# A graph network kernel on one core: TensorE enters the next pass inside the last steps of a pass, the last tile's weights are turned by TensorE, and passes 2 and 3 sum 256 columns

## The chip, the cores and the metric

One core of a Trainium2 chip. The metric is the device time of one execution, in microseconds (us). Three runs of the kernel before gave 2464.94, 2465.70 and 2465.91 us, median 2465.7 us.

## What is computed

Four graph layers over 6250 nodes with 128 features and 206250 edges. Every layer is normalised first and added to x (`layernorm` is over the features, without weights). Cut to what matters:

```
h = relu(layernorm(x));  x += segment_sum(w_edge * (sigmoid(h @ Wg + bg) * (h @ W0))[dst], src)
h = relu(layernorm(x));  x += segment_sum(h[src], dst) @ W1.T + b1
h = relu(layernorm(x));  m = [h[src], h[dst]] @ Wm + bm;  x += [h, segment_sum(m, dst)] @ Wu + bu
h = relu(layernorm(x));  e = Binv * segment_sum((h @ W3)[src], dst)
                         o = Dinv * segment_sum(e[dst], src) + b3
                         x += relu(gamma * batchnorm_over_nodes(o) + beta)
```

## The kernel before

The graph becomes a dense matrix of counts. The nodes are cut in 49 tiles of 128. **The build** makes, tile by tile, a 128 x 6272 strip of counts (how many edges go from node to node) and one of edge weights, by products of one-hot matrices on TensorE; ScalarE copies them from PSUM to `stage` (L1348 the counts and the high part of the weights, L1329 the low part of the weights). The counts are stored in DRAM (`counts_by_source`, 1.6 MB a tile). The weights of a tile (a high part and a low part, 49 blocks of 128 x 128 each) are turned into `wt` and multiplied with the gated rows `g_in`: this is layer 1, and it is done in the same stage, for a pair of tiles at a time (`sum_some`, L701 to L703, 16 groups of 3 target tiles, the last of 4; 3 matmuls of 128 columns for each target tile and source tile). VectorE adds each group into X (`add_some`, L1057).

**Four passes** then multiply the whole matrix of counts with rows of h: `step` on TensorE sums for each of the 49 tiles 49 matmuls (L804) of 258 columns: 128 of the high part of h, 128 of the low part and 2 extra ones (degrees). Pass 1 is layer 2, pass 2 layer 3, passes 3 and 4 layer 4. Only passes 1 and 4 read the two extra sums. Passes 1 to 3 load the counts of a tile with one DMA of 1.6 MB on the SP queue (L505, six slots, load j waits until tile j-6 is summed). Pass 4 needs the transposed matrix and loads two tiles at once with one DMA transpose (L542, three slots for pairs).

What orders the work around the change:

- The weights of tiles 0 to 47 are turned partly by DMA transposes on the SP queue (`hand_on`: L489, for each of the two parts a piece of 24 blocks and one of 17) and partly by TensorE (L725, 8 blocks a part, read out by ScalarE at L1358) inside the next tile's build. The last tile, 48, has no next tile, so all of its blocks go through the SP queue: L489 and then L499 (`rest_turned`). Its 147 matmuls are a group of their own (n = GROUPS - 1) behind the 294 of the pair ahead, and VectorE adds its 16 groups and takes the row statistics (`row_stats`, L1072) behind each.
- After the statistics come `norm` (L892 to L900), the split of h in two parts (L1286, L1101, L1103) and pass 1.
- A pass on TensorE is `tiles_loop(pe, step, 2)`: step j sums tile j, then turns the result of tile j-1 (L814, in pass 2 also L813), then multiplies that of tile j-2 with the layer's weights (L822; L825 and L826; L828). Steps 49 and 50 have only the latter two. ScalarE (`low`, `aggt`) and VectorE (`agg`, then X, the statistics and the next h, L1114 and L1124) follow; in passes 1 and 2 row j-5 of the next h is made at step j, so that VectorE and ScalarE have five more steps (49 to 53). The next pass begins when all 49 rows are there:

```
if ph > 1:
    pe.wait_ge(s(f"h_ready{ph}"), TILES)
```

- The sums of a pass alternate between PSUM banks 0 and 1 (`sum_bank`), and the two banks of tile 47 and 48 are free as soon as `low` and `agg` have read them.

## Time and profile before

| | |
|---|---|
| median of 3 runs | 2465.7 us (2464.94 to 2465.91) |
| profiled execution, its own time | 2461.69 us |
| its span | 2459.8 us |
| TensorE matmul busy | 2293.2 us, 93% |
| mean granted clock of TensorE | 0.978 of full speed |
| VectorE, ScalarE busy | 1444.7 us (59%), 1279.8 us (52%) |
| DMA moved | 569.80 MB, mean 232 GB/s |

The span is what the profiler's first and last instruction enclose; the execution's own time is 1.9 us more. In the span the build takes up to about 1234 us; pass 1 starts at 1241, pass 2 at 1541, pass 3 at 1864, pass 4 at 2137, and the last sum ends at 2435. "Busy" counts a matmul from its start to a modelled end, so that neighbours overlap; a rate is better read from start to start.

### The profile page before, as it was taken

The page shows a single profiled execution, that of the slowest core. Times are in us where ns is not written, and L with a number is a line of the kernel's source. Part 1 is how long each engine was busy: PE and PEld are TensorE (multiplying, and loading weights), DVE is VectorE, ACT ScalarE, POOL GpSimd, SP SyncE. Part 2 cuts the span into 40 slices and gives each one's busy share as a digit, 9 for nine tenths or more (in the row PEclk, how much of TensorE's full clock was granted, in tenths as well). Part 3 has the DMA queues.
Part 4 walks back from the last instruction along what each step waited for, and adds up shares of the span by engine and source line. Part 5 has one row for each costly group of instructions (what it writes and reads, how often), then busy time and mean ns, then how long its engine had stood idle before and what let it go on. Part 6 is the DMA issues. An engine that isn't in the chain of part 4 may idle for free.

```text
span 2459.8 us, 72172 instructions
## 1 busy us (share of the span) xinstructions
PE 2293.2 (93%) x28669; PEld 2025.0 (82%) x28669; DVE 1444.7 (59%) x3422; ACT 1279.8 (52%) x2875; POOL 57.0 (2%) x57
## 2 busy tenths in 40 slices
PE   3689999999999989999889998999998999998997
PEld 3469898998899889988768887888887888887886
DVE  8779999998899988989643233234333111222223
ACT  3689999999899989989342222222221000011112
POOL 3500000000000000000000000000000000000000
PEclk9799999999999999999989999999999999999998
DMA  7799999999999999999989999999998999999997
GB/s 188 182 213 195 201 212 207 209 210 200 189 208 208 196 203 195 205 197 205 226 202 291 290 290 290 248 261 257 258 261 214 291 290 290 264 252 241 269 268 188
DMA packets 1528563, 569.80 MB, mean 232 GB/s; under 512 B 869815, under 2 KB 1526971, under 8 KB 1528152
## 3 DMA queue, kind: packets, MB, share of 16 engines
q1 hardware_dynamic: 1524709, 559.04, 104.0%
q0 software_dynamic: 1200, 4.10, 0.6%
q8 instruction: 200, 3.28, 0.5%
q10 hardware_dynamic: 2370, 2.71, 0.4%
q14 instruction: 84, 0.68, 0.1%
HBM read 257.85 MB, written 92.19 MB: 142 GB/s over the span
## 4 chain that ended last, share of the span: by engine, by line
PE 63%; SPq 16%; ACT 9%; DMA 5%; issue 4%; DVE 3%; POOLq 1%; another core or an unknown queue 0%; POOL 0%; DVEq 0%; ACTq 0%
PE ps L804 35%; SPq L542 8%; SPq L489 5%; ACT stage L1348 4%; PE ps L732 4%; ACT stage L1329 3%; PE ps L733 3%; PE ps L734 3%; PE ps L701 3%; PE ps L702 3%; PE ps L703 3%; PE ps L709 3%; DMA wt<-stage 3%; SPq L486 2%; PE ps L725 1%
## 5 line engine op out<-in xcount | busy, mean ns | idle before, releaser
L1348 ACT CAST stage<-ps 128x784 f16<-128x784 f32 x784 | 657.4, 838 | 18.0 <-PE ps L734 10.5
L804 PE MATMUL ps<-Ha,a_tiles 128*128 128x258 f16 x4606 | 523.9, 273 | 7.2 <-DVE Ha L1124 7.2
L732 PE MATMUL ps<-hot_c,hot_r 128*128 128x98 f16 x3136 | 502.7, 210 | 13.5 <-DVE hot_c L1046 10.4
L804 PEld LDWEIGHTS ps<-Ha,a_tiles 128*128 128x128 f16 x4606 | 449.9, 98 | 73.5 <-DVE Ha L1124 7.6
L733 PE MATMUL ps<-hot_c,hot_r 128*128 128x98 f16 x3136 | 500.4, 210 | 0.0
L734 PE MATMUL ps<-hot_c,hot_r 128*128 128x98 f16 x3136 | 498.8, 209 | 0.0
L701 PE MATMUL ps<-g_in,wt 128*128 128x128 f16 x2401 | 426.9, 220 | 29.2 <-DMA wt<-stage 20.1
L1329 ACT CAST stage<-ps 128x392 f16<-128x392 f32 x784 | 405.1, 517 | 43.4 <-PE ps L709 40.8
L703 PE MATMUL ps<-g_in,wt 128*128 128x128 f16 x2401 | 426.9, 220 | 0.0
L702 PE MATMUL ps<-g_in,wt 128*128 128x128 f16 x2401 | 426.9, 220 | 0.0
L1046 DVE TENSOR_TENSOR hot_c<-hot_c,meta 128x1568 f16<-128x1568 f16 x392 | 379.2, 967 | 0.0
L732 PEld LDWEIGHTS ps<-hot_c,hot_r 128*128 128x128 f16 x3136 | 307.3, 98 | 42.3 <-ACT stage L1329 21.8
L733 PEld LDWEIGHTS ps<-hot_c,hot_r 128*128 128x128 f16 x3136 | 308.2, 98 | 13.9 <-issue 1.1
L734 PEld LDWEIGHTS ps<-hot_c,hot_r 128*128 128x128 f16 x3136 | 308.3, 98 | 0.0
L1057 DVE SCALAR_TENSOR_TENSOR X<-ps,X 128x384 f32<-128x384 f32 (+1 forms) x400 | 226.1, 565 | 111.5 <-PE ps L703 100.6
L804 PE MATMUL ps<-Hb,a_turned 128*128 128x258 f16 x2401 | 277.9, 274 | 12.6 <-DMA a_turned<-counts_by_source 10.5
L804 PE MATMUL ps<-Hb,a_tiles 128*128 128x258 f16 x2401 | 277.8, 274 | 6.9 <-DVE Hb L1124 6.9
L804 PEld LDWEIGHTS ps<-Hb,a_turned 128*128 128x128 f16 x2401 | 233.5, 98 | 50.1 <-DMA a_turned<-counts_by_source 13.6
L709 PE MATMUL ps<-stage,minus 128*128 128x392 f16 x784 | 259.5, 331 | 16.3 <-DVE hot_c L1046 9.7
L804 PEld LDWEIGHTS ps<-Hb,a_tiles 128*128 128x128 f16 x2401 | 234.9, 98 | 47.5 <-DVE Hb L1124 7.1
L1044 DVE TENSOR_TENSOR hot_r<-iota_r,meta 128x1024 f16<-128x1024 f16 x392 | 268.5, 685 | 0.0
L701 PEld LDWEIGHTS ps<-g_in,wt 128*128 128x128 f16 x2401 | 236.6, 99 | 34.4 <-issue 23.8
(199 smaller groups left out, 2338.6 us busy)
## 6 DMA issues: line engine op xcount, KB each, us to landing
a_tiles<-counts_by_source SPq DMA_DIRECT2D x147, 1600.0 KB, 13.2
counts_by_source<-stage SPq DMA_DIRECT2D x49, 1600.0 KB, 8.7
meta<-edge_groups SPq DMA_DIRECT2D x26, 128.0 KB, 2.4
wt<-stage SPq DMA_TRANSPOSE x198, 6.2
gated_parts<-G SPq DMA_DIRECT2D x7, 448.0 KB, 5.4
g_in<-gated_parts SPq DMA_DIRECT2D x98, 32.0 KB, 6.0
out_x<-X SPq DMA_DIRECT2D x12, 256.0 KB
edge_table<-tab ACTq DMA_DIRECT2D x1, 2040.0 KB, 10.6
```

The lines of the kernel that those rows point to most:

```text
L701: mm(o, at_[:, 0], g_in[:, c % 4, 0:P], start=i == tiles.start and b == 0, stop=False, skip_group_check=True)
L702: mm(o, at_[:, 0], g_in[:, c % 4, P:2 * P], start=False, stop=False, skip_group_check=True)
L703: last = mm(o, at_[:, 1], g_in[:, c % 4, 0:P], start=False, stop=True, skip_group_check=True)
L709: mm(o, minus16[:], stage[:, b, FULL:FULL + TILES, u * SET_COLS:(u + 1) * SET_COLS], start=False, stop=True, skip_group_check=True).then_i ...
L732: mm(into(0), rows_, codes(0), start=v == 0, stop=True, skip_group_check=True)
L733: mm(into(1), rows_, codes(1), start=v == 0, stop=False, skip_group_check=True)
L734: last = mm(into(1), rows_, codes(2), start=False, stop=True, skip_group_check=True)
L804: last = mm(ps[:, sum_bank(ph, j, c), 0:PARTS], a_slot(ph, c, i), moving[:, i], start=i == 0, stop=i == TILES - 1)
L1044: v.tensor_tensor(hot_r[:, b], iota_r[:].unsqueeze(1).to_broadcast([P, PAIRS, P, 2]), key(0, P), ALU.is_equal)
L1046: v.tensor_tensor(hot_c[:, b, :, 1:1 + WEIGHTS], hot_c[:, b, :, 0].unsqueeze(2).to_broadcast([P, PAIRS, WEIGHTS, WCOLS, 2]), weights[:, at ...
L1329: a.copy(stage[:, b, FULL + TILES:PARTED, u * SET_COLS:(u + 1) * SET_COLS], of).then_inc(s("lo_done"), 1)
L1348: a.copy(stage[:, b, 0:2 * FULL].rearrange("p (k i) d -> p k i d", k=2)[:, :, 0:TILES, u * SET_COLS:(u + 1) * SET_COLS], of).then_inc(s("h ...
```

## The change

- `tiles_loop` takes `written_out`: so many last steps are written out and not looped. Only `hand_on` on the SP queue uses it, with 12.
- The last tile's low parts (49 blocks) and the last 8 blocks of its high part are turned by TensorE: `LAST_TURNS`, 57 transposes in 8 lots, each lot in a PSUM bank of its own, read out by ScalarE with 8 copies into `wt`. The DMA transposes keep the high part's first 41 blocks; L499 goes. Both parts of `g_in` are loaded ahead of them.
- `last_sums` replaces the two rounds over the last pair and the last tile: groups 0 to 7 of the pair (tiles 46, 47) stay open in the eight banks, tile 48 is added to them, then groups 8 to 15 take all three tiles. VectorE adds 16 groups in place of 32, each with its row statistics.
- TensorE sums in passes 2 and 3 256 columns in place of 258 (`summed_cols`).
- At step 49 of passes 1 to 3 TensorE first sums 24 of the 49 matmuls of the next pass's tile 0, at step 50 the next 19 (`begin_next`), and behind step 50 (`end_first`) 43 of tile 1, then the last 6 of tile 0 one by one as the rows of h come, and the last 6 of tile 1. Bank numbers are shifted by the pass, so that tile 0 takes the bank of tile 47.

```diff
+AHEAD = (range(0, 24), range(24, 43))
...
+LAST_TURNS = ((0, 1, 0, 8), (0, 1, 8, 8), (0, 1, 16, 8), (1, 1, 0, 8), (1, 1, 8, 8), (1, 1, 16, 8), (1, 1, 24, 1), (1, 0, 17, 8))
...
+def summed_cols(ph):
+
+    return PARTS if ph in (1, 4) else 2 * P
...
-    return j if ph == 1 and isinstance(j, int) and j < TOGETHER else c % 2
+    return j if ph == 1 and isinstance(j, int) and j < TOGETHER else (c + ph - 1) % 2
...
+                        if isinstance(j, int) and j == TILES - 1:
+                            sp.dma_start(g_in[:, c % 4, P:2 * P], slab(g_dram, j)[:, P:2 * P]).then_inc(s(f"g_loaded{b}"), 16)
...
-                    turn(1, "lo_done", f"lo_turned{b}")
-
-                tiles_loop(sp, hand_on, 0)
...
+                    if not (isinstance(j, int) and j == TILES - 1):
+                        turn(1, "lo_done", f"lo_turned{b}")
+
+                tiles_loop(sp, hand_on, 0, LAP)
...
+                def last_sums():
+
+                    pe.wait_ge(s("lo_done"), TILES * HALVES)
+                    pe.wait_ge(s("added"), (GROUPS - 2) * SUMS)
+                    for r, (half, part, at_, n) in enumerate(LAST_TURNS):
+                        first = FULL + part * TILES + HALF_TILES[half].start + at_
+                        for x in range(n):
+                            last = tr(ps[:, r, x * P // 2:(x + 1) * P // 2].bitcast(F16), stage[:, 0, first + x], ident16[:])
+                        last.then_inc(s("pe_turned"), 1)
+                    loaded(GROUPS - 2, 0)
+                    loaded(GROUPS - 2, 1)
+                    for g in range(8):
+                        pe.wait_ge(s("turned_out"), (TILES - 1) * TURNS + g + 1)
+                        sum_into(g, g, (TILES - 3, TILES - 2), True)
+                    pe.wait_ge(s("hi_turned0"), GROUPS * 32)
+                    pe.wait_ge(s("g_loaded0"), GROUPS * 32)
+                    for g in range(8):
+                        sum_into(g, g, (TILES - 1,), False).then_inc(s("sum_made"), 1)
+                    for g in range(8, SUMS):
+                        pe.wait_ge(s("added"), (GROUPS - 2) * SUMS + g - 7)
+                        sum_into(g - 8, g, (TILES - 3, TILES - 2, TILES - 1), True).then_inc(s("sum_made"), 1)
...
+                def begin_next(ph, j):
+
+                    if j == TILES:
+                        counts_in(ph + 1, 0, 0)
+                        pe.wait_ge(s(f"low_ready{ph}"), TILES - 1)
+                        pe.wait_ge(s(f"agg_ready{ph}"), TILES - 1)
+                    pe.wait_ge(s(f"h_ready{ph + 1}"), AHEAD[j - TILES].stop)
+                    sum_tile(ph + 1, 0, 0, AHEAD[j - TILES])
+
+                def end_first(ph):
+
+                    counts_in(ph + 1, 0, 1)
+                    pe.wait_ge(s(f"low_ready{ph}"), TILES)
+                    pe.wait_ge(s(f"agg_ready{ph}"), TILES)
+                    sum_tile(ph + 1, 1, 1, range(AHEAD[1].stop))
+                    for i in range(AHEAD[1].stop, TILES):
+                        pe.wait_ge(s(f"h_ready{ph + 1}"), i + 1)
+                        sum_tile(ph + 1, 0, 0, (i,))
+                    sum_tile(ph + 1, 1, 1, range(AHEAD[1].stop, TILES))
...
+                        elif not on(j) and not general and ph < 4:
+                            begin_next(ph, j)
...
-                        if ph > 1:
-                            pe.wait_ge(s(f"h_ready{ph}"), TILES)
...
+                    if not general and ph < 4:
+                        end_first(ph)
...
+                    for r, (half, part, at_, n) in enumerate(LAST_TURNS):
+                        act.wait_ge(s("pe_turned"), (TILES - 1) * TURNS + r + 1)
+                        to = wt[:, home(TILES - 1, half), part, at_:at_ + n].rearrange("p i d -> p (i d)")
+                        a.copy(to, ps[:, r, 0:n * P // 2].bitcast(F16)).then_inc(s("turned_out"), 1)
```

How the order of the instructions moves. TensorE from the last step of pass 1 on, before (L804 are the sums, L814 and L822 the turning and the weights' product of finished tiles; "waits" names the semaphores):

```order
L804 MATMUL ps<-Ha,a_tiles 128x258 [waits agg_ready1,low_ready1,a_in0]
L804 MATMUL ps<-Ha,a_tiles 128x258 x48
L808 REGISTER_ALU
L814 MATMUL ps<-ident,agg 128x128 [waits aggt_ready1,agg_ready1]
L822 MATMUL ps<-w1t,aggt 128x128 [waits upd_done1,aggt_ready1]
L150 REGISTER_ALU
L150 COMPARE_AND_BRANCH
L814 MATMUL ps<-ident,agg 128x128 [waits aggt_ready1,agg_ready1]
L822 MATMUL ps<-w1t,aggt 128x128 [waits upd_done1,aggt_ready1] x2
L804 MATMUL ps<-Hb,a_tiles 128x258 [waits a_in1,h_ready2]
L804 MATMUL ps<-Hb,a_tiles 128x258 x48
```

And now, from the loop's end (its lines 808, 867 and 875 are the 804, 814 and 822 of before):

```order
L157 COMPARE_AND_BRANCH
L808 MATMUL ps<-Hb,a_tiles 128x256 [waits agg_ready1,h_ready2,low_ready1,a_in1]
L808 MATMUL ps<-Hb,a_tiles 128x256 x23
L867 MATMUL ps<-ident,agg 128x128 [waits aggt_ready1,agg_ready1]
L875 MATMUL ps<-w1t,aggt 128x128 [waits upd_done1,aggt_ready1]
L808 MATMUL ps<-Hb,a_tiles 128x256 [waits h_ready2]
L808 MATMUL ps<-Hb,a_tiles 128x256 x18
L875 MATMUL ps<-w1t,aggt 128x128 [waits upd_done1,aggt_ready1]
L808 MATMUL ps<-Hb,a_tiles 128x256 [waits agg_ready1,low_ready1,a_in2]
L808 MATMUL ps<-Hb,a_tiles 128x256 x42
L808 MATMUL ps<-Hb,a_tiles 128x256 [waits h_ready2] x6
L808 MATMUL ps<-Hb,a_tiles 128x256 x6
```

24 and 19 matmuls of the next pass have moved ahead of the two last products of this one, and 43 behind them; 12 are left that need the last rows of h.

The SP queue from the last tile of the build on, before (L489 and L499 turn weights, L493 stores the counts, L505 loads counts for pass 1):

```order
L486 DMA g_in<-gated_parts 128x128
L489 DMA_TRANSPOSE wt<-stage 128x24x128
L489 DMA_TRANSPOSE wt<-stage 128x17x128
L493 ISA
L493 DMA counts_by_source<-stage 128x25x256
L486 ISA [waits lo_done]
L486 DMA g_in<-gated_parts 128x128
L489 DMA_TRANSPOSE wt<-stage 128x24x128
L489 DMA_TRANSPOSE wt<-stage 128x17x128
...
L499 DMA_TRANSPOSE wt<-stage 128x8x128 x2
L505 DMA a_tiles<-counts_by_source 128x25x256 [waits hi_turned1,lo_turned1,turned_out,stored0,stored1]
```

And now:

```order
L493 DMA g_in<-gated_parts 128x128 [waits hi_done,sum_made]
L495 DMA g_in<-gated_parts 128x128
L498 DMA_TRANSPOSE wt<-stage 128x24x128
L498 DMA_TRANSPOSE wt<-stage 128x17x128
L502 DMA counts_by_source<-stage 128x25x256
L511 DMA a_tiles<-counts_by_source 128x25x256 [waits hi_turned1,lo_turned1,turned_out,stored0,stored1]
```

Four DMA transposes have left the queue; TensorE has 57 transposes (L721) between its last correction of counts (L739, before L709) and its first sum:

```order
L739 MATMUL ps<-stage,minus_51 128x392 [waits hi_done] x2
L721 MATMUL ps<-ident_52,stage 128x128 [waits added,lo_done]
L721 MATMUL ps<-ident_52,stage 128x128 x56
L703 MATMUL ps<-g_in,wt 128x128 [waits hi_turned1,turned_out,lo_turned1,g_loaded0,g_loaded1,lo_turned0,hi_turned0]
```

Nothing stood between the two before.

## Rows read from the trace of the kernel before

**Rows 1.** The page's chain that ended last: shares of the span by line.

```profile
PE ps L804 35%; SPq L542 8%; SPq L489 5%; ACT stage L1348 4%; PE ps L732 4%; ACT stage L1329 3%; PE ps L733 3%; PE ps L734 3%; PE ps L701 3%; PE ps L702 3%; PE ps L703 3%; PE ps L709 3%; DMA wt<-stage 3%; SPq L486 2%; PE ps L725 1%
```

**Rows 2.** Busy time by stretch: passes 2, 3 and 4; the last columns as headed.

```profile
core 0: us, PE busy (x) PEld busy (x) DVE busy (x) ACT busy (x) POOL busy (x), PEclk, DMA share, GB/s
1620.00:1840.00 220.00, 220.00 (x1907) 191.16 (x1905) 86.90 (x377) 58.58 (x174) 0.00 (x0) 1.00 1.00 260
2000.00:2110.00 110.00, 110.00 (x987) 95.98 (x985) 21.95 (x80) 5.54 (x20) 0.00 (x0) 1.00 1.18 290
2285.00:2415.00 130.00, 127.40 (x1131) 110.82 (x1130) 31.39 (x165) 16.96 (x88) 0.00 (x0) 1.00 1.20 268
```

**Rows 3.** TensorE's timeline at the three seams: start, us, engine, line, work [idle before].

```profile
1523.98 5.64 PE L804 MATMUL ps<-Ha,a_tiles 128*128 128x258 f16 x49
...
1540.67 12.68 PE L804 MATMUL ps<-Hb,a_tiles 128*128 128x258 f16 x98 [6.90 <-DVE Hb L1124]
...
1845.66 5.64 PE L804 MATMUL ps<-Hb,a_tiles 128*128 128x258 f16 x49
...
1864.48 15.69 PE L804 MATMUL ps<-Ha,a_tiles 128*128 128x258 f16 x123 [7.25 <-DVE Ha L1124]
...
2136.57 12.76 PE L804 MATMUL ps<-Hb,a_turned 128*128 128x258 f16 x98 [1.95 <-DVE Hb L1202]
```

**Rows 4.** Groups by line: the sums of passes 1 and 3, mean ns of one.

```profile
L804 PE MATMUL ps<-Ha,a_tiles 128*128 128x258 f16 x4606 | 523.9, 273 | 7.2 <-DVE Ha L1124 7.2
```

**Rows 5.** Granted clock (column PEclk) after the first seam.

```profile
1540.70:1544.00 3.30, 3.30 (x16) 2.33 (x17) 0.97 (x5) 0.00 (x0) 0.00 (x0) 0.51 1.19 288
```

**Rows 6.** Timeline of the end of the build: TensorE, ScalarE, VectorE.

```profile
1184.91 0.22 PE L701 MATMUL ps<-g_in,wt 128*128 128x128 f16 x1
...
1185.86 0.22 PE L703 MATMUL ps<-g_in,wt 128*128 128x128 f16 x1
...
1189.29 0.87 ACT L1329 CAST stage<-ps 128x392 f16<-128x392 f32 x2 [0.25 <-PE ps L709]
...
1216.12 0.56 DVE L1057 SCALAR_TENSOR_TENSOR X<-ps,X 128x384 f32<-128x384 f32 x1 [5.32 <-PE ps L703]
...
1231.70 0.67 DVE L1057 SCALAR_TENSOR_TENSOR X<-ps,X 128x512 f32<-128x512 f32 x1
...
1233.71 0.18 DVE L1138 MEMSET t<- 128x147 f32 x1
```

**Rows 7.** Groups by line: ScalarE's copy of counts out of PSUM.

```profile
L1348 ACT CAST stage<-ps 128x784 f16<-128x784 f32 x784 | 657.4, 838 | 18.0 <-PE ps L734 10.5
```

**Rows 8.** Line 489 from 1189.6: the last tile's high part on the SP queue.

```profile
L489 SPq DMA_TRANSPOSE wt<-stage x2: 2424/3064/3704, 1189.7 to 1193.5; - x2
...
DMA to landing us min/median/max: 4.7/5.2/5.7
```

**Rows 9.** VectorE's timeline at the seams: the last two rows of X.

```profile
1532.40 0.29 DVE L1220 TENSOR_TENSOR X<-X,ps 128x128 f32<-128x128 f32 x1
...
1534.25 0.28 DVE L1220 TENSOR_TENSOR X<-X,ps 128x128 f32<-128x128 f32 x1
...
1857.59 0.29 DVE L1227 TENSOR_TENSOR upd<-ps,bmu 128x128 f32<-128x128 f32 x1
```

**Rows 10.** Line 505, loads of pass 3: the first two, then the last 13.

```profile
L505 SPq DMA_DIRECT2D a_tiles<-counts_by_source x2: 368/368/368, 1871.9 to 1877.4; - x2
...
DMA to landing us min/median/max: 9.3/9.4/9.5
...
L505 SPq DMA_DIRECT2D a_tiles<-counts_by_source x13: 5052/5423/5699, 2036.3 to 2103.8; - x13
...
DMA to landing us min/median/max: 14.5/14.8/15.0
```

**Rows 11.** Line 542, the transposed loads of pass 4: all 25, and the first alone.

```profile
L542 SPq DMA_TRANSPOSE a_turned<-counts_by_source x25: 11539/11812/13551, 2118.2 to 2415.7; - x25
...
DMA to landing us min/median/max: 13.7/14.5/16.2
...
DMA to landing us min/median/max: 14.4/14.4/14.4
```

More of the change, by code:

```diff
@@ L149, in tiles_loop @@
         body(j, 0, j)
-    with eng.Fori(0, (TILES - peel) // LAP) as k:
+    with eng.Fori(0, (TILES - peel - written_out) // LAP) as k:
         for u in range(LAP):
             body(k * LAP + (peel + u), k * (LAP // SLOTS), peel + u)
-    for j in range(TILES, TILES + lag):
+    for j in range(TILES - written_out, TILES + lag):
         body(j, 0, j)
@@ L687, in layers, with sum_into @@
             def layers(general):
-                def sum_some(n, cp, g, both=True):
-                    f, e = n * SUMS + g, g % 2
-                    if not (isinstance(n, int) and n * SUMS + g < 2):
-                        pe.wait_ge(s("added"), f - 1)
+                def sum_into(bank, g, cs, begin):
                     half, tiles = int(g >= FIRST), summed(g)
                     for i in tiles:
-                        o = ps[:, 6 + e, (i - tiles.start) * P:(i - tiles.start + 1) * P]
-                        for b in range(1 + both):
-                            c = 2 * cp + b
+                        o = ps[:, bank, (i - tiles.start) * P:(i - tiles.start + 1) * P]
+                        for c in cs:
@@ L700, in sum_some @@
                             at_ = wt[:, home(c, half), :, i - HALF_TILES[half].start]
-                            mm(o, at_[:, 0], g_in[:, c % 4, 0:P], start=i == tiles.start and b == 0, stop=False, skip_group_check=True)
+                            mm(o, at_[:, 0], g_in[:, c % 4, 0:P], start=begin and i == tiles.start and c == cs[0], stop=False, skip_group_check=True)
                             mm(o, at_[:, 0], g_in[:, c % 4, P:2 * P], start=False, stop=False, skip_group_check=True)
                             last = mm(o, at_[:, 1], g_in[:, c % 4, 0:P], start=False, stop=True, skip_group_check=True)
-                    last.then_inc(s("sum_made"), 1)
+                    return last
@@ L802, in step @@
                                 pe.wait_ge(s(f"agg_ready{ph}"), j - 1)
-                            for i in range(TILES):
-                                last = mm(ps[:, sum_bank(ph, j, c), 0:PARTS], a_slot(ph, c, i), moving[:, i], start=i == 0, stop=i == TILES - 1)
-                            last.then_inc(s(f"sum_done{ph}"), 1)
+                            sum_tile(ph, j, c, range(TILES))
+                        elif not on(j) and not general and ph < 4:
+                            begin_next(ph, j)
                         if ph != 3 and on(j, 1):
@@ L1068, in row_stats @@
                 def row_stats(g):
[L1070 removed]
+                    dve.wait_ge(s("added"), SUMS * (GROUPS - 2) + g + 1)
                     for i in summed(g):
@@ L1089, in layers @@
                         add_some(GROUPS - 3, g)
-                    for n in (GROUPS - 2, GROUPS - 1):
-                        for g in range(SUMS):
-                            add_some(n, g)
-                            if n == GROUPS - 1 and g:
-                                row_stats(g - 1)
+                    for g in range(SUMS):
+                        add_some(GROUPS - 2, g, g % 8)
+                        if g:
+                            row_stats(g - 1)
                     row_stats(SUMS - 1)
```

58 lines of the change are left out of this document (28 added, 30 removed).

## The prediction

> **What bounds the kernel now.** I read the chain that ended last first: by line it is TensorE's sums (L804, 35% of the span) and, second, the SP queue in L542, the transposed loads of pass 4 (8%) [rows 1]. So passes 1 to 3 hang on TensorE and a part of pass 4 on DMA. The busy time by stretch says the same: in passes 2 and 3 TensorE has no gap (220.00 of 220.00 us, 110.00 of 110.00), but in pass 4 it is busy 127.40 of 130.00 us, and the DMA share, 1.00 in pass 2, is 1.18 in pass 3 and 1.20 in pass 4 [rows 2]. Then I read the seams: TensorE idles 6.90 us before pass 2, 7.25 before pass 3, 1.95 before pass 4 [rows 3]. Last, the end of the build: VectorE waits 5.32 us for the last tile's sums and then needs 17.6 us, from 1216.12 to 1233.71, for 16 adds with their statistics [rows 6]; the norm and pass 1 stand behind that.
>
> A matmul of 258 columns takes (5.64 - 0.27) / 48 = 0.1118 us from start to start [rows 3, 4], one of 128 columns (1185.86 - 1184.91) / 17 = 0.0559 us (18 matmuls of a group) [rows 6].
>
> **End of the build.** ScalarE's last low parts end at 1190.16 [rows 6]; there TensorE starts. 57 transposes at the price of a 128-column matmul: 3.2 us, to 1193.4. Groups 0 to 7 of the pair: 144 matmuls, 8.1 us, to 1201.4. ScalarE's copies run beside them: 1024 elements are bounded by the copy of 784 in 0.84 us [rows 7], in proportion 1.1 us; seven such and a small one end near 1199, each ahead of the group that wants it. The last tile's high part must have landed by 1201.4: its second DMA transpose was issued at 1193.5 and landed 4.7 us later, at 1198.2 [rows 8]; one small load more ahead of it adds 0.4. So nothing waits. Tile 48 into the eight banks: 72 matmuls, 4.0 us, to 1205.5; groups 8 to 15: 225 matmuls, 12.6 us, to 1218.1. VectorE beside it: from 1201.9 its 17.6 us end at 1219.5; behind TensorE's last sum it needs 2.0 us (1231.70 to 1233.71 [rows 6]) and 0.2 to get going, 1220.4. The later counts: 1220.4 in place of 1233.7, **13.3 us less**. What follows (norm, split) does not change. The loads of tiles 1, 2 and 0 come earlier, and those of 3 to 5 keep their place behind the adds.
>
> **Seam 1 to 2.** The last sum ends at 1523.98 + 5.48 = 1529.46 [rows 3]. 24 matmuls (2.7 us) now stand ahead of the turning of tile 48 and the product of tile 47, which end at about 1532.9; VectorE wanted the latter at 1532.40 [rows 9], so it is 0.6 us late. 19 more (2.1 us) put the product of tile 48 at 1535.4, where VectorE wanted it at 1534.25: 1.2 us late in all. So the last row of h comes at 1541.8, not 1540.67. Meanwhile TensorE does 43 matmuls (4.8 us, to 1540.1), those of tile 0 that are ready, waits about 1.1 us, ends tile 0 at 1542.0 and tile 1 at 1542.7. New is that the turning of tile 0 has no second whole tile in front of it: ScalarE and VectorE must read its sum first, VectorE behind its degrees, so tile 2 starts at 1543.9 after another idle us. Before it started at 1540.67 + 12.68 and its transposes, 1553.4. **9.4 us less.** 1.6 of them are clock: 98 matmuls should take 98 x 0.1118 and a tail of 0.16, 11.1 us, and took 12.7, because after the idle time the granted clock was 0.51, its lower level of 1.2 GHz [rows 5].
>
> **256 columns.** Between 128 and 258 columns the price rises (0.1118 - 0.0559) / 130 = 0.43 ns a column: 0.86 ns a matmul, 0.042 us a tile, 2.0 us over 47 tiles of a pass. In pass 2 **2.0 us less**. It could be 0, if a matmul's price went in steps, and no row excludes that.
>
> **Seam 2 to 3, pass 3 and the start of pass 4** go together, because DMA takes over. On TensorE: last sum at 1851.14; the same count puts the product of tile 48 at 1858.3, wanted at 1857.59 [rows 9]; the last row of h 0.7 us later, at 1865.2; tile 0 done at 1865.4, tile 2 starts at 1866.4 and not at 1877.2 (15.69 us for 123 matmuls from 1864.48, less 25 [rows 3]): 10.8 us, and 2.0 us by the columns, 12.8 us by the end of pass 3. But pass 3's loads came at 5.63 us each at the end (12 intervals from 2036.3 to 2103.8), slower than the 5.48 us in which TensorE sums a tile, and their landing grew from 9.3 to 14.8 us [rows 10]: DMA was full. Its work starts with load 6, when tile 0 is summed: 1871.9 before [rows 10], 1865.4 now. 9.3 us to the first landing and 42 times 5.63 give 2111.2 for the last, where it was 2103.8 and about 14.9, 2118.7: 7.5 us less. TensorE wants that load at 2116.4, so pass 3 itself runs free. The first transposed load may be issued when tile 45 is summed (now 2105.5), but it queues behind loads until 2111.2. Before it landed 2118.2 + 14.4 = 2132.6 [rows 11], 13.9 us behind the last load. Now, with its descriptors already queued, it may come 11.5 us (the shortest interval of L542) to 13.9 us behind: 7.5 to 9.9 us gained. I take the middle, **8.6 us**, as no row is nearer to either.
>
> **Pass 4.** Its 25 loads are issued without a break, 297.5 us from first to last for 24 intervals, 12.4 us each [rows 11], where TensorE needs 11.6 us for a pair. So the pass's end follows the first load, and the 3-to-4 seam (1.95 us idle and 1.6 us of low clock [rows 3]) is worth nothing: TensorE then waits for loads instead. Its own cover is the transfer. The Trainium skill ("Advanced Engine Details and Errata", section "X-Bar Transpose (TRN2)") says that "TRN2 transpose DMAs are as fast as regular DMAs". The trace disagrees: 11.8 us at the median for what two plain loads move in 11.3. By the page pass 4 would hang on TensorE, and all of the 12.8 us would count, 4.2 us more than in my sum.
>
> **Sum.** 13.3 + 9.4 + 2.0 + 8.6 = 33.3 us. The profiled execution took 2461.69 us, 4.0 below the median of 2465.7; from the median, 2432.4 us. A measurement of this kernel can tell about 0.2% (5 us) from no change.
>
> **Rivals.**
> - *Pass 4 keeps all that TensorE gains*, if loads and transposes overlap where I let them queue. For it: the first transposed load was issued before the last plain one had landed (2118.2 against 2118.7) and took no longer than the median. Against: the DMA share of 1.18 to 1.20. 37.5 us, 2428.2 us. Chance 0.12. The rule of the page above ends in the same time.
> - *The clock stays low in places.* The 1.95 us of idle before pass 4 cost 1.6 us (12.76 for 98 matmuls) [rows 3]; after the change two waits of about a us stand close together at the first seam, 1.4 us at the second, and 0.7 us at the build's end. Three such falls, 4.8 us: 2437.2 us. Against: all are shorter than 1.95. Chance 0.14.
> - *The change covers less than it says*: the tail of VectorE and ScalarE, steps 49 to 53, stretches by more than 1.2 us, or the last groups wait for a copy or for `wt`. With half of the seams' 18.0 us gone, 24 us remain: 2441.5 us. Chance 0.09.
> - *Slower*: the SP queue's last 12 steps are written out, and each must fetch its own instructions in a stage where TensorE waits for `wt`. In pass 4, whose first 13 steps are also written out, issues took up to 13.55 us against 11.54 at least [rows 11]: 2.0 us a step. It decides from (33.3 + 5) / 12 = 3.2 us a step on; the rows give at most 12 times 2.0, so this ends in a gain of 9 us unless it is worse than any row. At 4 us a step: 2480 us. Chance 0.02, and 0.01 for no change by it.
>
> **How the numbers follow.** My sum has 0.62. Its own range by the bounds (7.5 to 9.9 in pass 4, 0 to 2.0 for the columns, 1 to 2 us in each estimate of an idle time) is 2429 to 2437. With the two first rivals and the edge of the third: 2427 to 2441. Faster by over 0.2%: 0.97; within: 0.01; slower: 0.02.
>
> **What would show it.** Right: the last row statistics near 1220; pass 2's tile 2 near 1530 in the new trace's time; no plain gap of over 1.5 us on TensorE at the first two seams; load 6 of pass 3 some 14 us behind pass 2's last sum; the last plain load landing after the first L542 is issued; TensorE waiting for a_turned at nearly every pair; matmuls of 256 columns at 0.111 us. Wrong: pass 4 shorter than 297 us of loads, or VectorE's adds waiting for ScalarE's eight copies.

## The result, and the profile after

The changed kernel took 2424.91 us (median of 4 runs, 2424.05 to 2425.86), the kernel before on the same chip 2465.8 us (4 runs): a ratio of 0.9832, 95% interval 0.9815 to 0.9849. In a second set it was 2422.29 us (5 runs) against 2461.21 (9 runs), ratio 0.9841 [0.9827, 0.9855]. So it is 39 to 41 us faster. I had forecast 2432.4 with a range from 2427 to 2441: the direction was right and most terms were near, but the gain was 40.9 us for 33.3, and the time fell 2 us outside the range.

The profiled executions are 2461.69 us before and 2425.13 us after: 36.6 us apart, where the medians are 40.9 apart. The spans are 36.5 us apart, and I split those by events that both traces have ("last sum" is the start of a pass's last matmul):

| stretch | before | after | gained | forecast |
|---|---|---|---|---|
| start to the last correction of counts (L709, now L739) | 1189.09 | 1188.03 | 1.06 | 0 |
| to the end of the statistics | 44.62 | 31.17 | 13.45 | 13.3 |
| to pass 1's first sum (norm, split) | 7.51 | 7.51 | 0 | 0 |
| pass 1's tiles 0 to 3 | 27.27 | 26.11 | 1.16 | 0 |
| rest of pass 1, to its last sum's start | 260.86 | 260.87 | 0 | 0 |
| seam: to tile 2 of pass 2 | 24.06 | 13.87 | 10.19 | 9.4 |
| rest of pass 2 | 297.62 | 294.17 | 3.45 | 2.0 |
| seam, pass 3, start of pass 4, pass 4 | 584.13 | 577.07 | 7.06 | 8.6 |
| tail | 24.61 | 24.43 | 0.18 | 0 |
| sum | 2459.77 | 2423.23 | 36.54 | 33.3 |

The page of the profile after, its span, the busy time of TensorE, the chain by line, and three groups of instructions (they answer to [rows 1] and [rows 4]; line 804 is 808 now, 542 is 548):

```profile
span 2423.3 us, 72160 instructions
...
PE 2277.8 (94%) x28726; PEld 2018.4 (83%) x28726; DVE 1436.6 (59%) x3406; ACT 1286.1 (53%) x2883; POOL 53.9 (2%) x57
...
PE ps L808 33%; SPq L548 9%; SPq L498 5%; ACT stage L1400 4%; PE ps L703 3%; PE ps L762 3%; ACT stage L1381 3%; PE ps L705 3%; PE ps L704 3%; PE ps L763 3%; PE ps L764 3%; DMA wt<-stage 3%; PE ps L739 3%; DMA a_turned<-counts_by_source 2%; SPq L493 2%
...
L808 PE MATMUL ps<-Ha,a_tiles 128*128 128x256 f16 (+1 forms) x4606 | 519.6, 273 | 1.6 <-DVE Ha L1176 1.5
...
L808 PE MATMUL ps<-Hb,a_turned 128*128 128x258 f16 x2401 | 277.9, 274 | 17.4 <-DMA a_turned<-counts_by_source 17.1
...
L808 PE MATMUL ps<-Hb,a_tiles 128*128 128x256 f16 x2401 | 273.1, 272 | 0.9 <-DVE Hb L1176 0.9
```

The sums have lost two points of the chain and the transposed loads have gained one. TensorE's idle time before the sums fell from 6.9 and 7.2 us to 0.9 and 1.6 in passes 2 and 3; that before `a_turned` rose from 10.5 us, in the row of the kernel before below, to 17.1 us. The seams' idle time has partly come back as a wait for DMA.

```profile
L804 PE MATMUL ps<-Hb,a_turned 128*128 128x258 f16 x2401 | 277.9, 274 | 12.6 <-DMA a_turned<-counts_by_source 10.5
```

The timelines of the end of the build and of the seams, over TensorE, ScalarE and VectorE (start, us, engine, line, work, idle before; they answer to [rows 3, 6]):

```profile
1188.23 0.87 ACT L1381 CAST stage<-ps 128x392 f16<-128x392 f32 x2 [0.25 <-PE ps L739]
...
1189.16 3.36 PE L721 MATMUL ps<-ident,stage 128*128 128x128 f16 x57 [0.79 <-ACT stage L1381]
...
1189.82 6.68 ACT L1422 COPY wt<-ps 128x1024 f16<-128x1024 f16 x8 [0.71 <-PE ps L721]
...
1217.17 0.69 DVE L1110 SCALAR_TENSOR_TENSOR X<-ps,X 128x512 f32<-128x512 f32 x1 [0.87 <-PE ps L705]
...
1219.20 0.18 DVE L1190 MEMSET t<- 128x147 f32 x1
...
1519.42 5.46 PE L808 MATMUL ps<-Hb,a_tiles 128*128 128x256 f16 x48
1525.80 0.94 PE L808 MATMUL ps<-Hb,a_tiles 128*128 128x256 f16 x7 [0.92 <-DVE Hb L1176]
1527.28 0.33 PE L866 MATMUL ps<-ident,hrow 128*128 128x128 f32 x1 [0.54 <-DVE agg L1243]
...
1527.56 5.57 PE L808 MATMUL ps<-Hb,a_tiles 128*128 128x256 f16 x49
...
1834.70 0.28 PE L808 MATMUL ps<-Ha,a_tiles 128*128 128x256 f16 x1 [0.37 <-DVE Ha L1176]
1836.08 10.16 PE L808 MATMUL ps<-Ha,a_tiles 128*128 128x256 f16 x88 [1.10 <-DVE Ha L1176]
...
2093.76 12.69 PE L808 MATMUL ps<-Hb,a_turned 128*128 128x258 f16 x98 [2.33 <-DMA a_turned<-counts_by_source]
```

To be read here: the 57 transposes begin right behind ScalarE's last low part (1188.23 + 0.87, after 0.79 us of idle time on TensorE) and take 3.4 us; the eight copies end at 1196.5, ahead of every group that needs one; VectorE's last add starts once TensorE's last sum is there, and adds and statistics end 2.0 us later. At the first seam two short waits of 0.92 and 0.54 us are left of 6.90, at the second 0.37 and 1.10 of 7.25. At the third the wait is no shorter (2.33 for 1.95), and what ends it has changed from VectorE's last row of h to the first transposed load.

The busy time by stretch: pass 2, pass 3, pass 4 in two parts, and 3.3 us behind the first seam (the columns of [rows 2]):

```profile
1600.00:1820.00 220.00, 220.00 (x1929) 192.99 (x1928) 88.78 (x385) 58.53 (x176) 0.00 (x0) 1.00 1.01 262
1960.00:2070.00 110.00, 110.00 (x1000) 97.06 (x998) 21.94 (x80) 5.72 (x21) 0.00 (x0) 1.00 1.18 290
...
2095.00:2256.00 161.00, 148.53 (x1308) 128.56 (x1306) 34.52 (x185) 18.64 (x97) 0.00 (x0) 0.99 1.24 252
2260.00:2385.00 125.00, 121.22 (x1071) 104.90 (x1070) 30.16 (x158) 16.24 (x84) 0.00 (x0) 1.00 1.19 266
...
1526.70:1530.00 3.30, 2.76 (x26) 2.42 (x26) 0.69 (x3) 1.12 (x4) 0.00 (x0) 1.00 1.19 290
```

The granted clock stays at 1.00 behind the first seam, where it was 0.51 [rows 5]. Pass 3 moves 290 GB/s, as before. New to me is the difference between the two parts of pass 4: 252 GB/s while its first steps run, 266 afterwards. The kernel before has it too: 251 GB/s from 2140 to 2285 us, 268 from there to 2415.

The loads of pass 3 behind the first six, and the 25 transposed loads, by line (duration of the issue min/median/max, first and last start; they answer to [rows 10, 11]):

```profile
L511 SPq DMA_DIRECT2D a_tiles<-counts_by_source x43: 368/5372/6160, 1836.4 to 2067.8; - x43
...
DMA to landing us min/median/max: 8.0/14.8/15.5
```

```profile
L548 SPq DMA_TRANSPOSE a_turned<-counts_by_source x25: 11663/11955/16126, 2075.2 to 2379.3; - x25
...
DMA to landing us min/median/max: 14.0/14.9/18.5
```

Load 6 of pass 3 goes 35.5 us earlier, the last plain one 35.9 (2103.8 to 2067.8), the first transposed load 43.0 (2118.2 to 2075.2). It is issued 7.1 us before the last plain load lands, and takes 18.5 us itself: at 2093.7 in place of 2132.6, 38.9 us earlier. The last transposed load is issued only 36.4 us earlier (2415.7 to 2379.3). Pass 4 gave 2.5 us of the gain back.

### The profile page after: what moved, and what is told of

Its sections match the earlier page's. It is cut to its first block, busy times and chain, and to the rows that moved or that the text cites. A ratio compares the mean times of both kernels' runs of the same rounds, so it can differ in the third digit from the quotient of the medians.

```text
span 2423.3 us, 72160 instructions
## 1 busy us (share of the span) xinstructions
PE 2277.8 (94%) x28726; PEld 2018.4 (83%) x28726; DVE 1436.6 (59%) x3406; ACT 1286.1 (53%) x2883; POOL 53.9 (2%) x57
## 4 chain that ended last, share of the span: by engine, by line
PE 61%; SPq 17%; ACT 9%; DMA 7%; issue 3%; DVE 2%; POOLq 0%; POOL 0%; ACTq 0%; DVEq 0%
PE ps L808 33%; SPq L548 9%; SPq L498 5%; ACT stage L1400 4%; PE ps L703 3%; PE ps L762 3%; ACT stage L1381 3%; PE ps L705 3%; PE ps L704 3%; PE ps L763 3%; PE ps L764 3%; DMA wt<-stage 3%; PE ps L739 3%; DMA a_turned<-counts_by_source 2%; SPq L493 2%
## 5 line engine op out<-in xcount | busy, mean ns | idle before, releaser
L1400 ACT CAST stage<-ps 128x784 f16<-128x784 f32 x784 | 656.0, 837 | 21.2 <-PE ps L764 13.7
L808 PE MATMUL ps<-Ha,a_tiles 128*128 128x256 f16 (+1 forms) x4606 | 519.6, 273 | 1.6 <-DVE Ha L1176 1.5
L762 PE MATMUL ps<-hot_c,hot_r 128*128 128x98 f16 x3136 | 502.3, 210 | 18.7 <-DVE hot_c L1098 13.3
L703 PE MATMUL ps<-g_in,wt 128*128 128x128 f16 x2401 | 422.4, 219 | 16.3 <-DMA wt<-stage 12.7
L705 PE MATMUL ps<-g_in,wt 128*128 128x128 f16 x2401 | 422.8, 219 | 0.0
L704 PE MATMUL ps<-g_in,wt 128*128 128x128 f16 x2401 | 422.6, 219 | 0.0
L763 PEld LDWEIGHTS ps<-hot_c,hot_r 128*128 128x128 f16 x3136 | 308.1, 98 | 13.9 <-issue 0.9
L808 PE MATMUL ps<-Hb,a_turned 128*128 128x258 f16 x2401 | 277.9, 274 | 17.4 <-DMA a_turned<-counts_by_source 17.1
L1110 DVE SCALAR_TENSOR_TENSOR X<-ps,X 128x384 f32<-128x384 f32 (+1 forms) x384 | 217.0, 565 | 106.5 <-PE ps L705 96.1
L739 PE MATMUL ps<-stage,minus 128*128 128x392 f16 x784 | 259.8, 332 | 15.7 <-DVE hot_c L1098 10.2
L808 PE MATMUL ps<-Hb,a_tiles 128*128 128x256 f16 x2401 | 273.1, 272 | 0.9 <-DVE Hb L1176 0.9
```

Source lines behind the costliest of these rows:

```text
L703: mm(o, at_[:, 0], g_in[:, c % 4, 0:P], start=begin and i == tiles.start and c == cs[0], stop=False, skip_group_check=True)
L704: mm(o, at_[:, 0], g_in[:, c % 4, P:2 * P], start=False, stop=False, skip_group_check=True)
L705: last = mm(o, at_[:, 1], g_in[:, c % 4, 0:P], start=False, stop=True, skip_group_check=True)
L739: mm(o, minus16[:], stage[:, b, FULL:FULL + TILES, u * SET_COLS:(u + 1) * SET_COLS], start=False, stop=True, skip_group_check=True).then_i ...
L762: mm(into(0), rows_, codes(0), start=v == 0, stop=True, skip_group_check=True)
L763: mm(into(1), rows_, codes(1), start=v == 0, stop=False, skip_group_check=True)
```

## The experiments

All were run with their own runs of the kernel before beside them. Medians move from set to set (those of the kernel before were 2460.2 to 2465.8 us), so I read differences of a few us from the traces, from one event to another, where the build's scatter is left out. "Behind the counts" is the time from the last correction of counts to the end of the span: 1270.7 us for the kernel before, 1235.2 us for the changed one (1234.9 in its second profile). Two of its parts scatter from one profile to another, whatever the kernel: pass 1's tiles 0 to 3 take 25.9 to 27.3 us, and pass 2's last sum to pass 4's last takes 575.7 to 577.1 us in the changed kernel's two profiles, in `seam34_old` and in `build_old`.

**The third seam as before** (`seam34_old`).

```diff
-                        elif not on(j) and not general and ph < 4:
+                        elif not on(j) and not general and ph + 1 not in (1, 4, 5):
...
+                    elif ph > 1 and ph in (1, 4, 5):
+                        pe.wait_ge(s(f"h_ready{ph}"), TILES)
```

> The changed kernel with the seam between passes 3 and 4 as before: TensorE sums nothing of pass 4 until all rows are there. Theory 1 (DMA carries the time from the sixth load of pass 3 to the end of pass 4, so this seam is under the first transposed load): 2425 us, within 1 us of the changed kernel; its trace shows TensorE starting pass 4 when the first transposed load lands, near 2093.8 us. Rival (each seam is worth what TensorE idles in it): the idle 1.95 us and 1.6 us of low clock come back, 2428.5 us.

Measured: 2427.37 us, ratio 0.9848 [0.9828, 0.9868]; 1235.2 us behind the counts, as with the third seam changed. TensorE starts pass 4 with the same wait:

```profile
2097.46 6.72 PE L808 MATMUL ps<-Hb,a_turned 128*128 128x258 f16 x44 [2.40 <-DMA a_turned<-counts_by_source]
```

The median lies nearer to the rival's 2428.5 than to 2425, but from the last correction of counts on, where the edit acts, no time is lost; from pass 2's last sum to pass 4's it is 576.0 us, for 577.1 and 576.0 in the changed kernel. So the third seam is worth nothing within the scatter of a us: the first transposed load covers it.

**All three seams as before** (`seams_old`): the same edit for every pass.

```diff
-                        elif not on(j) and not general and ph < 4:
+                        elif not on(j) and not general and ph + 1 not in (1, 2, 3, 4, 5):
...
+                    elif ph > 1 and ph in (1, 2, 3, 4, 5):
+                        pe.wait_ge(s(f"h_ready{ph}"), TILES)
```

> The changed kernel with all three seams as before; the end of the build and the 256 columns stay changed. Theory 1: lost are 10.2 us at the first seam (25.9 us ahead at tile 2 of pass 2, 15.7 at the last sum of pass 1) and 9.6 us at the second (38.9 us ahead at the first transposed load's landing, 29.3 at the last sum of pass 2), nothing at the third: 2444.7 us. Rival (the third counts too): 2448 us. Rival 2 (DMA is not full in pass 3, the second seam is worth all that TensorE gains, 11.0 us): 2446 us with the first transposed load landing 14.4 us behind the end of tile 45.

Measured: 2441.27 us, ratio 0.9918 [0.9902, 0.9934]; 1249.2 us behind the counts, 14.0 more than the changed kernel. None of the three expected times was met; the nearest, 2444.7, had 9.6 us for the second seam. The first seam is 10.9 us of the 14.0 (24.81 for 13.87). The second costs TensorE 11.4 us (26.83 for 15.41), but only 3.3 are left at the end of pass 4 (580.4 us from pass 2's last sum, for 577.1; 4.4 against the second profile). On TensorE, by the timeline, the wait before pass 4 is a wait for h again:

```profile
1522.51 13.46 PE L808 MATMUL ps<-Hb,a_tiles 128*128 128x256 f16 x98 [6.88 <-DVE Hb L1178]
...
2113.26 1.96 PE L808 MATMUL ps<-Hb,a_turned 128*128 128x258 f16 x16 [1.95 <-DVE Hb L1256]
```

and its first transposed load is issued 3.1 us before the last plain one lands, not 7.1, and lands 14.6 us later, not 18.5:

```profile
L548 SPq DMA_TRANSPOSE a_turned<-counts_by_source x1: 12172/12172/12172, 2095.1 to 2095.1; - x1
...
DMA to landing us min/median/max: 14.6/14.6/14.6
```

From pass 2's last sum the issue is 11.4 us later and the load's last packet 7.4; and from there the other 24 loads need 294.9 us where the changed kernel's need 299.1 (by their packets too; 297.8 in its second profile). 7.4 less 4.2 are about the 3.3. The early entry into pass 3 is real on TensorE and is mostly eaten by DMA.

**258 columns again** (`cols258`).

```diff
-    return PARTS if ph in (1, 4) else 2 * P
+    return PARTS
```

> The changed kernel with 258 columns in passes 2 and 3. Theory 1 (DMA carries pass 3, so only pass 2 counts): the 3.45 us that pass 2 gained in the trace from its tile 2 to its last sum come back, 2428.4 us. Rival (both passes count): 2431.8 us. By the linear price of my prediction, pass 2 alone, 2426.9 us.

Measured: 2429.52 us, ratio 0.9861 [0.9842, 0.9881]; 1239.0 us behind the counts, 3.8 more. Pass 2 is 3.45 us longer, as much as the change took from it. Pass 3 is longer too, but from pass 2's last sum to the end of pass 4 it is 576.8 us, against 577.1 and 576.0: what pass 3 saves is worth nothing here. The two don't add, though. The kernel before, which has the old seams and 258 columns, needs 584.1 us, 3.7 more than with the old seams alone. In the old order the first transposed load follows TensorE, which frees its place at tile 45: its last packet comes 1.8 us earlier behind pass 2's last sum with 256 columns (279.1 us) than with 258, and that is what pass 3's columns gain there. The other 2 us are the 24 loads behind it, and they scatter by nearly as much.

**254 and 240 columns** (`cols_less`, one run, 2420.93 us).

```diff
-    return PARTS if ph in (1, 4) else 2 * P
+    return {1: PARTS, 2: 254, 3: 240, 4: PARTS}[ph]
```

> The changed kernel with 254 columns in pass 2 and 240 in pass 3, which leaves out the last features' low parts there. 258 columns took 111.8 ns a matmul, 256 took 110.3, 128 took 55.9. Theory 1 (a matmul goes by its columns, at 0.43 ns each): 109.4 ns in pass 2 and 103.4 in pass 3. Theory 2 (a step: 256 and less cost one thing, above it another): 110.3 in pass 2. Pass 3 stays bound by its loads (5.63 us a tile), so that TensorE waits there.

Measured: from start to start inside a row of them a matmul takes, in the mean over the pass, 111.8 ns at 258 columns, 110.3 at 256, 108.9 at 254 and 102.5 at 240. One tile of pass 2, here and in the changed kernel above, is 5.50 and 5.57 us, and 5.64 with 258:

```profile
1702.41 5.50 PE L808 MATMUL ps<-Hb,a_tiles 128*128 128x254 f16 x49
```

There is no step at 256. Between 254 and 258 a column costs 0.72 to 0.75 ns, between 240 and 254 0.46, between 128 (55.9 ns) and 240 0.42. In pass 3 TensorE is idle 8% of the time, while DMA moves what it moved before (stretch inside pass 3, columns of [rows 2]):

```profile
1960.00:2070.00 110.00, 100.82 (x955) 90.64 (x953) 21.63 (x79) 5.55 (x20) 0.00 (x0) 1.00 1.19 290
```

Its loads run at the old pace, 231.6 us from the issue of load 6 to that of the last, against 231.5. DMA, not TensorE, sets pass 3's pace.

**SP's last steps written out, alone** (`before_written`, on the kernel before).

```diff
-    with eng.Fori(0, (TILES - peel) // LAP) as k:
+    with eng.Fori(0, (TILES - peel - written_out) // LAP) as k:
...
-                tiles_loop(sp, hand_on, 0)
+                tiles_loop(sp, hand_on, 0, LAP)
```

> The kernel before with one thing changed: the SP queue's last 12 steps of the build are written out. Theory 1: no effect, within 1 us of the kernel before. Rival A (the 1.1 us by which the changed kernel's build ended earlier, at TensorE's last correction of counts, come from there): 1 us less. Rival B (each written-out step costs its own instruction fetch, up to 2.0 us a step): up to 24 us more.

Measured: 2462.49 us (12 runs), ratio 0.9991 [0.9979, 1.0003]. No effect that can be told from none; the slower rival falls.

**The end of the build as before** (`build_old`): seams and columns of the changed kernel, the last tile by the old way.

```diff
-                tiles_loop(sp, hand_on, 0, LAP)
+                tiles_loop(sp, hand_on, 0)
+                for a in range(WEIGHTS):
+                    first = FULL + a * TILES + TURN_FIRST
...
-                    last_sums()
+                    for n in (GROUPS - 2, GROUPS - 1):
...
```

> The changed kernel with the end of the build as before (last tile through the SP queue, two rounds of sums and adds, the SP loop's last steps not written out). Theory 1: the end of the build is worth what the trace shows between the last correction of counts and the statistics, 44.6 against 31.2 us: 13.4 us more, 2438.4 us. Theory 2: a part of it is given back in pass 1, where loads must be there earlier and the clock after the wait falls for another time: 10 us or less, 2435 us or under.

Measured: 2436.13 us, ratio 0.99 [0.9885, 0.9915]; 13.5 us more behind the counts. The stretch to the statistics is 44.22 us in place of 31.17, 13.05 more, and pass 1's first four tiles take 27.10 in place of 26.11. The latter is scatter and no gain of the new end: the same tiles take 26.78 us in the changed kernel's second profile and 27.12 in `seam34_old`, both with the new end, and 25.95 in `before_written`, with the old one. Nor is the low clock at this place longer with the old end as such: it lasts 13.7 us here and in the kernel before, but 10.2 us in `before_written` and `before_lap6`, as with the new end. Of the 13 us nothing is seen to be given back later; the median, 2436.13, lies between the two expected times, and the trace decides.

**Pass 3 loads less** (`light3`).

```diff
-                    sp.dma_start(a_tiles[:, q].rearrange("p (i a) d -> p i (a d)", a=2), two_tiles(j)).then_inc(s(f"a_in{q}"), 16)
+                    pairs = 22 if ph == 3 else FULL // 2
+                    sp.dma_start(a_tiles[:, q, 0:2 * pairs].rearrange("p (i a) d -> p i (a d)", a=2), two_tiles(j)[:, 0:pairs]).then_inc(s(f"a_in{q}"), 16)
```

> Pass 3 loads 22 of the 25 pairs of blocks of each tile, so 12% less; part of the counts is old data, so the result of layer 4 isn't the reference's. Theory 1 (DMA is full in pass 3 and its last load opens pass 4): the loads keep to TensorE's pace of 5.40 us a tile, the landing stays near 9 to 10 us, and the first transposed load, issued as soon as tile 45 is summed, lands about 14.4 us later, 3 to 5 us earlier than now: 2421 us. Theory 2 (transposed loads take up where TensorE ends, the price is the last tile's): no change, 2425 us.

Measured: 2418.89 us, ratio 0.9832 [0.9816, 0.9848]; 1228.0 us behind the counts, 7.2 less than the changed kernel. The loads no longer pile up:

```profile
L512 SPq DMA_DIRECT2D a_tiles<-counts_by_source x43: 367/373/3611, 1837.8 to 2060.5; - x43
...
DMA to landing us min/median/max: 7.0/7.5/13.0
```

```profile
L549 SPq DMA_TRANSPOSE a_turned<-counts_by_source x1: 11710/11710/11710, 2076.6 to 2076.6; - x1
...
DMA to landing us min/median/max: 14.0/14.0/14.0
```

An issue takes 0.37 us at the median and not 5.37. The first transposed load is issued at the same distance behind the counts (887.6 us, for 887.2) and lands 14.0 us later, not 18.5. By its last packet that is 4.2 us, within what theory 1 wanted; the other 3.0 us are the 24 loads behind it (296.1 us for 299.1, but 297.8 in the changed kernel's second profile). The full queue of pass 3 is what opens pass 4 those 4 us late.

**Loops of 6 steps** (`lap6`). By the end of each transposed pair's packets (I cut the trace's 256-byte packets into 24.5 equal parts), of the changed kernel's first 13 intervals between pairs nine are 13.0 to 13.8 us and four 11.9 to 12.6, and the later ones 12.0 to 12.2, but for one of 12.7. In the first part the DMA view shows instruction packets between them, in the second none:

```profile
q1 hardware_dynamic: 158424, 40.46, 123.3%
q8 instruction: 10, 0.16, 0.4%
q14 instruction: 3, 0.02, 0.0%
...
q1 hardware_dynamic: 130467, 33.31, 119.5%
```

Pass 4 has 13 steps written out and then the loop's first round of 12, all new code, so I made the rounds 6 and the steps ahead of them 7.

```diff
-    peel = LAP + 1
+    peel = lap + 1
...
-                    tiles_loop(sp, step, 0)
+                    tiles_loop(sp, step, 0, lap=SLOTS)
...
-                        tiles_loop(pe, step, 2)
+                        tiles_loop(pe, step, 2, lap=SLOTS)
```

(VectorE and ScalarE the same.)

> The loops of the four passes are written out 6 steps at a time in place of 12, and 7 first steps stand ahead of them in place of 13. In the changed kernel the first 13 pairs of pass 4 are 13.5 us apart while engines still fetch instructions that they run for the first time (packets of 16 KB on a queue of their own), the later ones 12.1 to 12.2. Theory 1: these fetches, or the code that is new, slow the transposed loads; half of the slow pairs become fast: 6 or 7 times 1.3 us, about 8 us less, 2417 us. Theory 2: the slow pairs come from which tiles they read, whatever the engines fetch: 2425 us, and the slow pairs remain 13.

Measured: 2417.07 us, ratio 0.9829 [0.9816, 0.9843]; 1227.9 us behind the counts, 7.3 less. Pass 4 alone, from pass 3's last sum, is 300.2 us for 307.7. TensorE's wait for `a_turned` fell from 17.1 to 9.6 us, and the median of an issue from 11.96 to 11.74 us:

```profile
L548 SPq DMA_TRANSPOSE a_turned<-counts_by_source x25: 11482/11743/15948, 2074.3 to 2371.1; - x25
...
  PE ps L808: 9.6, 10
```

The slow stretch ends with the last instruction packet of the new code, at 2180 and not 2256 (two stretches of lap6, columns of [rows 2]; clock, DMA share and GB/s are the last three):

```profile
2095.00:2180.00 85.00, 79.30 (x685) 68.14 (x684) 17.72 (x95) 9.55 (x49) 0.00 (x0) 0.97 1.25 255
2185.00:2375.00 190.00, 187.15 (x1666) 163.36 (x1665) 46.92 (x242) 25.03 (x128) 0.00 (x0) 1.00 1.19 268
```

The traces say more: it is not new code as such, but each instruction packet by itself. Over all fourteen traces, 126 intervals between pairs with a 16 KB instruction packet in them are 13.3 us in the mean, and 191 with none are 12.2 (five with one of 8 KB alone: 12.4). Inside the slow stretch of the changed kernel the two intervals without a packet are 11.9 us. In its second profile, and in `light3`, a lone packet comes at 2324 and 2321 us, 80 us behind the others, and just that interval is 13.5 and 13.4 us among neighbours of 12.2 and 12.3. The DMA view of it (GB/s in slices of 0.2 us, `after_again` from 2320 to 2328 us) has a hole of 1.2 us at 10 GB/s and less, right behind the packet:

```profile
GB/s 291 291 293 287 291 289 291 291 293 287 291 289 291 291 293 287 291 289 291 291 293 362 273 271 92 8 0 6 8 10 9 79 291 288 289 291 292 291 291 288
...
q8 instruction: 1, 0.02, 0.9%
```

Such holes (at least 0.3 us in which less than 35 GB/s arrive) stand, with 0.5 to 1.4 us each, behind all 14 instruction packets of pass 4 in the changed kernel (two packets share one) and add up to 14.0 us; in lap6 six of its seven packets have one, 6.7 us in all. The difference is as large as the 7.3 us gained (the second profiles have 13.9 and 6.4 us of holes, for 5.4 us gained). The bytes cannot be it: 16 KB at 268 GB/s would be 0.06 us, an estimate.

**The same on the kernel before** (`before_lap6`).

> The kernel before, with the loops of the four passes written out 6 steps at a time in place of 12 as in lap6. Theory 1: the slow pairs of pass 4 come from instruction fetches in both kernels; before has 12 of them, 5 or 6 become fast, and pass 4 is 6 to 8 us shorter: 0.30% under the kernel before. Theory 2: only the changed kernel, in which TensorE waits for nearly every pair, can gain by it: before gains under 3 us.

Measured: 2455.49 us, ratio 0.9968 [0.9956, 0.9981], 5.5 us less by the medians and 4.7 to 10.8 by the interval. In the trace pass 4 is 3.7 us shorter (297.1 for 300.8), between the two theories. The loops cost the kernel before something too; that it is less than in the changed kernel only the traces say, and their 24 loads scatter by 1 to 2 us.

**Without the 50th block** (`no_pad6`, on lap6; TensorE's waits count two DMAs a tile).

```diff
-                    sp.dma_start(a_tiles[:, q].rearrange("p (i a) d -> p i (a d)", a=2), two_tiles(j)).then_inc(s(f"a_in{q}"), 16)
+                    whole = TILES // 2
+                    sp.dma_start(a_tiles[:, q, 0:2 * whole].rearrange("p (i a) d -> p i (a d)", a=2), two_tiles(j)[:, 0:whole]).then_inc(s(f"a_in{q}"), 16)
+                    sp.dma_start(a_tiles[:, q, TILES - 1:TILES], two_tiles(j)[:, whole:whole + 1, 0:P]).then_inc(s(f"a_in{q}"), 16)
```

> lap6, and passes 1 to 3 load 49 blocks of a tile (24 pairs and one block alone, in two DMAs) and not the 50th, which nothing reads. Theory 1: pass 3's loads go by bytes; 2% less, 0.11 us of 5.63 a tile, 42 times: the last load lands up to 4.7 us earlier, and so does pass 4: 4 us under lap6. Theory 2: they go by packets, and a packet of 256 bytes takes as long as one of 512; then nothing is gained, and a second DMA for every tile costs 0 to 2 us: the same as lap6.

Measured: 2417.38 us, ratio 0.9825 [0.9809, 0.9841], the same as lap6 by the medians; in the trace 2.0 us less behind the counts (1225.9 for 1227.9), and pass 3's last load lands 2.9 us earlier, counted from pass 2's last sum. That is about half of what theory 1 wanted (4 and 4.7), too little to call it faster.

**The changed kernel and lap6 side by side.**

> The changed kernel once more, beside lap6 on the same chip, because the kernel before gave medians from 2460.2 to 2465.8 us at different times and the ratios of the changed kernel (0.9832) and of lap6 (0.9829) can't be told apart. Theory 1 (the trace's 7.3 us of lap6 are real): a ratio of 0.983 to 0.986, and lap6 0.003 lower. Theory 2 (lap6 gives nothing in most executions): both ratios equal within 0.001.

> lap6 once more beside the changed kernel. Theory 1: 6 to 9 us under the changed kernel's median of the same call, and the pass 4 of its profile again 7 us shorter. Theory 2: within 2 us of it.

Measured: 2422.29 us (5 runs, 0.9841 [0.9827, 0.9855]) and 2416.21 us (5 runs, 0.9817 [0.9801, 0.9832]): lap6 is 6.1 us under the changed kernel, and pass 4 is 5.5 us shorter in the profile (301.1 for 306.6), a little under theory 1's 7. The intervals overlap a little; what settles it is that the 24 loads behind the first pair take 294.9 to 299.1 us in the ten profiles with loops of 12 (of both kernels), and 291.9 to 293.3 in the four with loops of 6. lap6 is the version that beats both kernels.

## Why the prediction was right, and what failed

- **The base, the step that failed most:** "from the median, 2432.4 us". The base itself held: the kernel before gave 2465.8 us beside the changed one. What failed is that the sum took nothing to change ahead of the last correction of counts, and that the range had nothing for the scatter there. From the medians, less 1.9 us outside the span and the 1270.7 and 1235.2 us behind the counts, I estimate 1193.2 us for that part before and 1187.8 after: 5.4 us for a forecast of 0. The second set gives 3.1 us, the two profiles above 1.06. I took three runs that lay within 1 us as a sign of little scatter; later sets gave medians of 2464.2, 2460.2, 2461.0 and 2461.2 us, with single runs from 2457.1 to 2469.5. Whether the 5.4 us are all scatter stays open: in the three profiles of the kernel before and its two variants the last correction comes at 1189.1 to 1195.7 us, in the eleven of the changed kernel and its variants at 1185.1 to 1190.6, `build_old` with the old end among them (1187.2), and no run isolates a cause. `before_written` shows that SP's written-out steps are not it.
- **End of the build**: 13.3 forecast, 13.45 in the trace, 13.05 with that part alone undone. Right, and nothing waits: TensorE goes from the first transpose to the last sum without a gap, and so neither for ScalarE's copies nor for `wt`. The 1.16 us at pass 1's first tiles, which the sum had at 0, are scatter (`build_old` above).
- **Seam 1 to 2**: 9.4 forecast, 10.2 measured, 10.9 with the seams alone undone. The two waits were forecast at 1.1 and 1 us and took 0.92 and 0.54.
- **256 columns**: 2.0 forecast, 3.45 measured. The price of 0.43 ns a column was mis-sized: the last columns cost 0.75 ns each. The line between 128 and 258 was right in the mean and wrong at its end.
- **Seam 2 to 3, passes 3 and 4**: 8.6 forecast, 7.1 measured. On TensorE the seam is the forecast 10.8 us. That pass 3 is bound by its loads held (light3, cols_less). Its last load was forecast 7.5 us earlier, from a landing reckoned with 5.63 us a load (2111.2) set against one read off (2118.7); reckoned alike, the kernel before has 2117.7, a gain of 6.5, and 6.6 was measured. The first pair lands 11.3 us behind the last plain load, just under my lower bound of 11.5, and in the kernel before it was 14.4, not 13.9. The two slips cancel: the first pair gained 9.6 us, inside my 7.5 to 9.9. Then 2.5 were lost in pass 4, which I had taken as unchanged at 12.4 us a pair. Part of these 2.5 is scatter: the same 24 loads took 1.3 us less in the changed kernel's second profile.
- **Seam 3 to 4**: worth nothing, as forecast (seam34_old).
- **Rivals.** Pass 4 did not keep TensorE's gain: of 13.9 us at the last sum of pass 3 (12.8 forecast) 7.1 arrived. That rival's time, 2428.2, is nearer to the result than mine, and for the wrong reason. The rule of the Trainium skill ("Advanced Engine Details and Errata", section "X-Bar Transpose (TRN2)"), that transposes are as fast as regular DMAs on TRN2, does not hold in these traces either: 12.2 us a pair in the mean where no instruction packet falls, against 11.3 for two plain loads of the same bytes together. The clock did the opposite of my rival: waits of up to 1.1 us at the first two seams did not lower it, and the stretches at 1.2 GHz that stood behind both in the kernel before (10.2 us each) are gone. Waits of 1.95 to 3.1 us before pass 4 stand in ten profiles; 3.4 us of low clock followed in seven of them, and none in three (1.95 to 2.03 us). The seams' gain was not halved, and SP's written-out steps cost nothing.

Behind the counts the differences from the forecast are +0.15, +1.16 (scatter), +0.79, +1.45, -1.54 and +0.18 us: 33.3 becomes 35.5. The other 5.4 us of the 40.9 lie ahead of the counts, by the estimate above. Without those the time would have been 2430 us, inside the range; that it would be so near is in part luck, as the terms missed to both sides.

What stays open: how an instruction packet of 16 KB stops the transposed loads for up to 1.4 us; the traces show the hole behind it and not its reason. Open too is whether the kernel before gains less by `lap6`, and why: the holes shrink there by 6.2 us (12.3 to 6.1), pass 4 by 3.7.

## What to carry to other kernels

Entering the next pass with the rows of h that are ready wins the whole seam only where TensorE sets the pace; where loads run full behind it, ask when the first load of the next stage lands, since that is all that arrives. Anchor a forecast and an experiment on an event inside the trace and give the runs' own scatter a place in the range: here three runs within 1 us hid a scatter of 5.6 us between sets, as large as a term of the sum. In a stage bound by DMA, count the instruction packets, and so the code that is executed for the first time: halving the loop bodies brought 6.1 us by the medians (5.4 and 7.3 behind the counts), nearly as much as all that arrived of the second and third seams with pass 3 (7.1 us).
